# Graph attention: the larger slope moved from exponentials to VectorE, one exponential in place, and shares scaled on ScalarE

## The chip, the cores and the metric

The kernel is one program on one core of a Trainium2 chip. Its metric is the device time in microseconds (us) of one execution. It is a whole network in one launch; the change touches one stage, the attention of the first graph layer.

## The reference, cut to what matters

The first graph layer has 12 heads of 64 values, 1250 nodes and 20,000 edges. For every edge it takes a score `a1[src] + a2[dst]`, a leaky ReLU with slope 0.2, a softmax over the edges that end in one node, and the sum of the source nodes' values by these weights.

```python
ft = jnp.einsum('nhd,ed->nhe', hh, W_fc)
a1 = jnp.einsum('nhd,hd->nh', ft, attn_l)
a2 = jnp.einsum('nhd,hd->nh', ft, attn_r)
e = jax.nn.leaky_relu(a1[src] + a2[dst], negative_slope=NEG_SLOPE)
m = jax.ops.segment_max(e, dst, num_segments=n)
ee = jnp.exp(e - m[dst])
denom = jax.ops.segment_sum(ee, dst, num_segments=n)
alpha = ee / denom[dst]
agg = jax.ops.segment_sum(alpha[:, :, None] * ft[src], dst, num_segments=n)
res = jnp.einsum('nhd,ed->nhe', hh, W_res)
return jax.nn.relu((res + agg).reshape(n, H * D))
```

Behind it come a mixture of experts, two more graph layers and a transformer block, none of which the change touches.

## The kernel before

The edges are kept as a dense table of counts, `counts_u`, source by destination. The nodes make 10 tiles of 125 (`TP`), so a step `i` is one head and one tile of 125 sources against all 1250 destinations: 12 x 10 = 120 steps, in order of heads. The function is `attend_narrow`; its queues are written out by hand, one for each engine, with semaphores between them.

For each step, ScalarE makes two exponentials of 125x1250, one for each slope of the leaky ReLU (lines 1709 and 1710): the row of the destinations plus a bias for each source, `ks` for the slope 1 and `ks_low` for the slope 0.2. Since the exponential rises, the larger of the two results is the exponential of the leaky ReLU. VectorE takes that larger one (`larger`, line 1722), then limits it to 1 and multiplies it by the counts (line 1742). TensorE multiplies the weights by the values with a column of ones (65 columns in all, line 1674), in three pieces of up to 512 destinations, and adds up over the 10 steps of a head in PSUM (`acc`). VectorE's loop takes the larger one of step i+1 before it weighs step i.

The sums of a head are divided by their last column one head later. ScalarE copies them out of PSUM (`copy_sums`, after step 3 of the next head), TensorE turns them by 10 transposes (`turn_sums`, after step 5, line 1662), and VectorE does the rest after step 7 in `take_out`: it adds 1e-16 (1728), inverts (1730), scales all 10 tiles in one instruction (1731) and adds the shares to the result (1735). The last head's sums go the same way behind the last step.

Buffers: 5 for the high slope, 4 for the low one. Two heads' rows and the exponentials of the first two steps are made ahead, in the stage before (`EarlyHeads`). SyncE loads the rows of head h once the exponentials of head h-2 are done, and between them issues 39 fills of zeros for a later stage.

Of the kernel before, what the change touches and what calls it, by code (L numbers as in the profile page):

```python
# [12 lines left out]
ALU = mybir.AluOpType  # L13
ACT = mybir.ActivationFunctionType
# [1536 lines left out]
class EarlyHeads:  # L1551
# [8 lines left out]
    def __init__(self, s, g, tag, ks, ks_low):  # L1560
        self.g, self.ks, self.ks_low = g, ks, ks_low
        G = self.HEADS
        self.rows_all = [s.sb(f"{tag}_rows{i}", [P, 2, N]) for i in range(G)]
        self.lowb_all = [s.sb(f"{tag}_lowb{i}", [P, N]) for i in range(self.STEPS)]
        self.shifted = s.sb(f"{tag}_early_shifted", [TP, NT, 2, G])
        masks = g.far_u[:, :, :].rearrange("p t n -> p (t n)").bitcast(F32)
        self.high = [masks[:, i * N:(i + 1) * N] for i in range(NT // 2)]
# [38 lines left out]
def attend_narrow(g, tag, ks, ks_low, shifted, ft, res, early):  # L1606
# [3 lines left out]

    H = ks.shape[2]
    WIDTH = ft.shape[3]
    DV = WIDTH - 1
    pieces = [(0, 512), (512, 1024), (1024, N)]
    steps = [(h, t) for h in range(H) for t in range(NT)]

    COPY, TURN, TAKE = 3, 5, 7
    HALF = NT // 2  # L1620
    with ExitStack() as ctx:
        s = Scope(g, ctx)
        rows_all = early.rows_all
        rows = [x[0:TP, :, :] for x in rows_all]

        shiftedT = s.sb(f"{tag}_shiftedT", [2 * H, N])[:, :]

        high = early.high
        lowb = [x[0:TP, :] for x in early.lowb_all] + [s.sb(f"{tag}_lowb{i}", [TP, N])[:, :] for i in range(early.STEPS, 4)]
        HB, LB = len(high), len(lowb)  # L1630
# [7 lines left out]
        exp_done, max_done, wts_done = early.exp_done, s.sem(f"{tag}_max"), s.sem(f"{tag}_wts_done")  # L1638
        multiplied, sums_out, sums_turned = s.sem(f"{tag}_multiplied"), s.sem(f"{tag}_sums_out"), s.sem(f"{tag}_sums_turned")
        taken, v_chain = s.sem(f"{tag}_taken"), s.sem(f"{tag}_vc")  # L1640
# [6 lines left out]
        wts = high  # L1647

        @block.tensor
        def _(pe):  # L1650
            for t in range(NT):
                last = pe.transpose(acc[1][0:2 * H, t // 4, (t % 4) * TP:(t % 4 + 1) * TP],
                                    shifted[:, t, :, :].rearrange("p a c -> p (a c)"), g.ident[0:TP, 0:TP])
            last.then_inc(turned, 1)

            def turn_sums(h):
                pe.wait_ge(sums_out, h + 1)
                if h >= 1:

                    pe.wait_ge(taken, h)  # L1660
                for d in range(NT):
                    last = pe.transpose(back[:, d // HALF, (d % HALF) * WIDTH:(d % HALF + 1) * WIDTH],
                                        sumsT[:, d * TP:(d + 1) * TP], g.ident[0:WIDTH, 0:WIDTH])
                last.then_inc(sums_turned, 1)

            for i, (h, t) in enumerate(steps):
                if t == 0 and h == 1:
                    pe.wait_ge(copied, 2)
                if t == 0 and h >= 2:

                    pe.wait_ge(sums_out, h - 1)
                pe.wait_ge(wts_done, i + 1)
                for b, (c0, c1) in enumerate(pieces):
                    last = pe.matmul(acc[h % 2][0:WIDTH, b, 0:c1 - c0], ft[:, t, h, :], wts[i % HB][:, c0:c1],  # L1674
                                     start=(t == 0), stop=(t == NT - 1))
                last.then_inc(multiplied, 1)
                if t == TURN and h >= 1:
                    turn_sums(h - 1)
            turn_sums(H - 1)

        @block.scalar
        def _(act):
            def copy_shifted():
                act.wait_ge(turned, 1)
                act.activation(shiftedT[:, 0:8 * TP].rearrange("p (a b) -> p a b", a=2), acc[1][0:2 * H, 0:2, 0:4 * TP],
                               ACT.Copy).then_inc(copied, 1)
                act.activation(shiftedT[:, 8 * TP:N], acc[1][0:2 * H, 2, 0:2 * TP], ACT.Copy).then_inc(copied, 1)

            def copy_sums(h):
                act.wait_ge(multiplied, (h + 1) * NT)  # L1690
# [6 lines left out]
            for i, (h, t) in enumerate(steps):  # L1697
                if i < early.STEPS:
                    continue
                if i == early.STEPS + 4:  # L1700
                    copy_shifted()
                if t == 0:
                    act.wait_ge(rows_in[h % 2], h // 2 * 16 + 16)
                if i >= HB:

                    act.wait_ge(multiplied, i - HB + 1)
                if i >= LB:
                    act.wait_ge(max_done, i - LB + 1)
# [3 lines left out]
                if t == COPY and h >= 1:  # L1712
                    copy_sums(h - 1)
            copy_sums(H - 1)

        @block.vector
        def _(dve):
            link = chain(dve, v_chain)

            def larger(i):  # L1720
                dve.wait_ge(exp_done, i + 1)
                dve.tensor_tensor(high[i % HB], high[i % HB], lowb[i % LB],  # L1722
                                  op=ALU.max).then_inc(max_done, 1)

            def take_out(h):
                dve.wait_ge(sums_turned, h + 1)
                by_tile = back[:, :, 0:HALF * WIDTH].rearrange("p a (d w) -> p a d w", w=WIDTH)
                link(dve.tensor_scalar(recip[:, :].rearrange("p (a d) -> p a d", a=2), by_tile[:, :, :, DV], 1e-16, None,
                                       op0=ALU.add))
                link(dve.reciprocal(recip[:, :], recip[:, :]))  # L1730
                link(dve.tensor_tensor(shares[:, :, :].rearrange("p (a d) w -> p a d w", a=2), by_tile[:, :, :, 0:DV],
                                       recip[:, :].rearrange("p (a d) -> p a d", a=2).unsqueeze(3)
                                       .to_broadcast([TP, 2, HALF, DV]), op=ALU.mult))
                at = slice(h * DV, (h + 1) * DV)
                dve.tensor_tensor(res[:, :, at], res[:, :, at], shares[:, :, :], op=ALU.add).then_inc(taken, 1)

            larger(0)
            for i, (h, t) in enumerate(steps):
                if i + 1 < len(steps):
                    larger(i + 1)  # L1740
                dve.wait_ge(max_done, i + 1)
                dve.scalar_tensor_tensor(out=wts[i % HB], in0=high[i % HB], scalar=1.0,  # L1742
                                         in1=g.counts_u[:, t, :], op0=ALU.min, op1=ALU.mult).then_inc(wts_done, 1)
                if t == TAKE and h >= 1:
                    take_out(h - 1)
            take_out(H - 1)
            dve.wait_ge(taken, H)

        @block.sync
        def _(sp):  # L1750
# [1 line left out]
            sp.dma_start(g.rows_dram[0:2 * H, :], shiftedT).then_inc(rows_out, 16)  # L1752
            sp.wait_ge(rows_out, 16)
            for h in range(early.HEADS, H):
                sp.wait_ge(exp_done, (h - 1) * NT)
# [268 lines left out]
def gat_layer(g, x, src, dst, etype, w_fc, w_res, attn_l, attn_r, layers, weights):  # L2024
# [9 lines left out]
    with ExitStack() as ctx:  # L2034
# [6 lines left out]
        with ExitStack() as inner:  # L2041
# [8 lines left out]
            early = EarlyHeads(si, g, "gat2", ks, ks_low)  # L2050
            with ExitStack() as inmost:
                sm = Scope(g, inmost)
                row = [x[:, :].unsqueeze(1) for x in early.lowb_all] + [sm.sb("gat_row2", [P, 1, N])[:, :, :]]
# [1367 lines left out]
```

## Time and profile before

| | us |
|---|---|
| time, median of 3 runs | 3122.57 |
| the three runs | 3122.57, 3121.82, 3135.45 |
| the profiled execution: its span, first to last instruction | 3130.0 |
| the attention stage in it, VectorE's first to last instruction | 489.91 to 849.41 |

The profile gives the span of its execution and no separate whole time. Only the longest of the three runs is longer than that span, by 5.4 us; the median lies 7.4 us under the span.

How to read the views: a row of the groups gives the line, the engine, what is written from what, the shape, the count, then busy us and the mean ns of one, then the engine's idle time just before these instructions and what ended it. PE is TensorE's matmul, DVE VectorE, ACT ScalarE. PEclk is TensorE's granted clock as a share of its higher level.

### The profile page before, as it was taken

To read this page: it belongs to the slowest core of one execution; us is meant where nothing else is said; L and a number is where in the kernel's file an instruction comes from. 1 tells how busy PE (TensorE), PEld (TensorE's weight loads), DVE (VectorE), ACT (ScalarE), POOL (GpSimd) and SP (SyncE) were. 2 spreads that over 40 slices of the span, in tenths; PEclk is the share of its full clock that TensorE was granted. 3 is DMA by queue.
4 is the path that set the end of the run, shared out by engine and by line. 5 is a ranking of instruction groups with operands and counts; after the bars stand their busy time and mean duration, and the time that the engine had idled before them with its cause. 6 is when DMAs were issued, how large, how long until landed. Compare 5 with 4: busy or idle time off the path is not lost. (4 is left out here: it accounts for less than half of the span.)

```text
span 3130.0 us, 34859 instructions
## 1 busy us (share of the span) xinstructions
PE 2710.3 (87%) x12638; PEld 2001.7 (64%) x12639; DVE 2038.7 (65%) x2833; ACT 1247.1 (40%) x1499; POOL 293.7 (9%) x148
## 2 busy tenths in 40 slices
PE   7877986888766983999999996999999799999979
PEld 3556982333235981555999995998887655566654
DVE  6765999999853544893888995705677871114451
ACT  1573227889520001111777782225655610004310
POOL 0000000000025853000000001510000000000020
PEclk9998558999867996999999997999999899999979
DMA  1566544211026635542665543625343601000031
GB/s 66 145 176 150 167 147 176 88 49 50 0 75 196 206 135 186 191 147 109 187 175 158 132 113 104 193 79 182 120 130 111 194 14 61 31 5 26 1 90 50
DMA packets 155542, 361.24 MB, mean 115 GB/s; under 512 B 27292, under 2 KB 77924, under 8 KB 154634
## 3 DMA queue, kind: packets, MB, share of 16 engines
q1 hardware_dynamic: 110468, 269.91, 28.6%
q10 hardware_dynamic: 35968, 73.97, 6.8%
q0 software_dynamic: 8960, 15.41, 1.9%
q8 instruction: 93, 1.52, 0.2%
q14 instruction: 53, 0.43, 0.0%
HBM read 276.26 MB, written 82.93 MB: 115 GB/s over the span
## 5 line engine op out<-in xcount | busy, mean ns | idle before, releaser
L1674 PE MATMUL gat_acc<-far_u,gat_ft 125*65 125x512 f32 x720 | 286.7, 540 | 56.1 <-DVE far_u L1742 55.6
L1674 PEld LDWEIGHTS gat_acc<-far_u,gat_ft 125*65 125x65 f32 x720 | 94.1, 142 | 244.9 <-issue 152.8
L1134 PE MATMUL rg_out<-rg_w,rg_hT 128*125 128x384 f32 x720 | 234.3, 489 | 0.0
L2263 PE MATMUL rg2a_acc<-rg2a_value_part,rg2a_wts_part 125*125 125x512 f32 x600 | 204.9, 342 | 14.8 <-DVE rg2a_wts_part L1983 11.4
L2264 PE MATMUL rg2a_acc<-rg2a_value_part,rg2a_wts_part 125*125 125x512 f32 x600 | 205.7, 343 | 0.0
L2265 PE MATMUL rg2a_acc<-rg2a_value_part,rg2a_wts_part 125*125 125x512 f32 x600 | 204.1, 340 | 0.0
L1134 PEld LDWEIGHTS rg_out<-rg_w,rg_hT 128*125 128x125 f32 x720 | 135.8, 189 | 97.4 <-issue 1.5
L1722 DVE TENSOR_TENSOR far_u<-far_u,gat_lowb 125x1250 f32<-125x1250 f32 x120 | 174.3, 1453 | 0.4 <-PEq L782 0.4
L1742 DVE SCALAR_TENSOR_TENSOR far_u<-far_u,counts_u 125x1250 f32<-125x1250 f32 x120 | 174.3, 1453 | 0.0
L1709 ACT ACTIVATE far_u<-gat_rows,gat_ks 125x1250 f32<-125x1250 f32 x118 | 156.7, 1328 | 43.2 <-PE gat_acc L1674 34.2
L365 PE MATMUL sums<-src_hot,key_hot 125*125 125x512 bf16 (+1 forms) x618 | 139.4, 355 | 30.0 <-DVE key_hot L300 28.6
L1710 ACT ACTIVATE gat_lowb<-gat_rows,gat_ks_low 125x1250 f32<-125x1250 f32 x118 | 156.3, 1325 | 0.0
L299 DVE TENSOR_SCALAR src_hot<-number,srcT 125x1250 bf16<-125x1250 uint16 x206 | 112.5, 546 | 44.6 <-PE sums L365 27.0
L1980 DVE TENSOR_TENSOR rg2a_value_part<-rg2a_values,rg2a_value_part 125x770 fp32r<-125x770 f32 x89 | 85.5, 961 | 77.7 <-ACT rg2a_value_part L1933 76.9
L2263 PEld LDWEIGHTS rg2a_acc<-rg2a_value_part,rg2a_wts_part 125*125 125x125 f32 x600 | 112.9, 188 | 30.6 <-DVE rg2a_value_part L1980 12.0
L2263 PE MATMUL rg_out<-rg_w,rg_hT 128*125 128x384 f32 x360 | 123.0, 342 | 8.0 <-POOL rg_w L1210 8.0
L365 PEld LDWEIGHTS sums<-src_hot,key_hot 125*125 125x125 bf16 x618 | 72.4, 138 | 84.9 <-DVE key_hot L300 65.0
L1417 PE MATMUL rg1a_acc<-rg_values,rg1a_high 125*125 125x193 f32 x720 | 122.4, 327 | 3.7 <-DVE rg1a_high L1496 1.9
L1417 PE MATMUL rg1a_acc<-rg1a_values,rg1a_high 125*125 125x193 f32 x720 | 122.1, 327 | 1.7 <-DVE rg1a_high L1496 0.9
L2265 PE MATMUL rg_out<-rg_w,rg_hT 128*125 128x384 f32 x360 | 122.6, 340 | 0.0
L2264 PE MATMUL rg_out<-rg_w,rg_hT 128*125 128x384 f32 x360 | 122.5, 340 | 0.0
L2265 PEld LDWEIGHTS rg2a_acc<-rg2a_value_part,rg2a_wts_part 125*125 125x125 f32 x600 | 113.1, 189 | 14.2
(481 smaller groups left out, 6014.7 us busy)
## 6 DMA issues: line engine op xcount, KB each, us to landing
rg2a_values<-values_dram SPq DMA_DIRECT2D x89, 384.0 KB, 3.4
rg1a_counts<-counts_dram SPq DMA_DIRECT2D x26, 820.3 KB
rg_mask<-far_dram SPq DMA_DIRECT2D x60, 312.5 KB, 3.6
moe_raw<-in_L_ffn_w SPq DMA_DIRECT2D x16, 1152.0 KB, 5.8
relw_chunk<-in_L_gnn_W ACTq DMA_DIRECT2D x36, 384.0 KB, 3.1
gat_rows<-rows_dram SPq DMA_DIRECT2D x10, 1250.0 KB, 5.7
sorted_dram<-gat_zeros SPq DMA_DIRECT2D x30, 384.0 KB, 9.4
values_dram<-rg_stage ACTq DMA_DIRECT2D x30, 384.0 KB, 2.3
```

Of the source, the lines that this page charges most:

```text
L299: dve.tensor_scalar(src_hot[u][:, :], number[:, 0:N], srcT[:, bass.ds(t, 1)], None, op0=ALU.is_equal)
L365: last = pe.matmul(sums_flat[b][:, 512 * k:512 * k + w], key_hot[u][:, :], src_hot[u][:, 512 * k:512 * k + w], start=start, stop=False, sk ...
L1134: last = pe.matmul(self.out_ps[n % 2][:, a, 0:384], self.hT[:, c, t * TP:(t + 1) * TP], self.w_sb[r % 2][:, c, a * 384:(a + 1) * 384], sta ...
L1417: last = pe.matmul(tile_of(h, d), wts[i % HB][:, d * TP:(d + 1) * TP], stream[i % VB][:, :], start=first and d % 2 == 0, stop=final, skip_ ...
L1674: last = pe.matmul(acc[h % 2][0:WIDTH, b, 0:c1 - c0], ft[:, t, h, :], wts[i % HB][:, c0:c1], start=(t == 0), stop=(t == NT - 1))
L1709: act.activation(high[i % HB], rows[h % 2][:, 0, :], ACT.Exp, bias=ks[:, t, h:h + 1])
L1710: act.activation(lowb[i % LB], rows[h % 2][:, 1, :], ACT.Exp, bias=ks_low[:, t, h:h + 1]).then_inc(exp_done, 1)
L1722: dve.tensor_tensor(high[i % HB], high[i % HB], lowb[i % LB], op=ALU.max).then_inc(max_done, 1)
L1742: dve.scalar_tensor_tensor(out=wts[i % HB], in0=high[i % HB], scalar=1.0, in1=g.counts_u[:, t, :], op0=ALU.min, op1=ALU.mult).then_inc(wts ...
L2263: pe.matmul(out, still[0], moving[0], start=first, stop=False)
L2264: pe.matmul(out, still[0], moving[1], start=False, stop=False)
L2265: return pe.matmul(out, still[1], moving[0], start=False, stop=final)
```

## The change

Four things are done together.

- VectorE now makes the exponent: for each step it adds `ks_high` = 0.8 x `ks` to the high row, by a pointer scalar (one value for each partition), and takes the larger of that and the low row (`exponents`). ScalarE makes one exponential of it, in place, with the bias `ks_low`, instead of two.
- Two steps make a pair. The counts are multiplied over the pair in one instruction of 125x2500, and TensorE is told of a pair at a time, so there are 60 pairs, 5 for each head. The ring has 4 buffers of a pair. The first pair's exponentials are still those made ahead.
- The scaling of the sums moves from VectorE (one instruction of 125x640, line 1731) to ScalarE: ten copies from PSUM of 64 columns each, with a pointer scale (`share`). `take_out` is parted into `invert`, after pair 3 of the next head, and the addition, after pair 4. ScalarE's `share` stands after the exponentials of pair 3 in its queue.
- The places are counted in pairs: the sums are copied after pair 1, turned after pair 2.

SyncE's wait before a row load is now on VectorE's exponents, since it is VectorE that reads the rows.

```diff
-        high = early.high
-        lowb = [x[0:TP, :] for x in early.lowb_all] + [s.sb(f"{tag}_lowb{i}", [TP, N])[:, :] for i in range(early.STEPS, 4)]
+        ks_high = s.sb(f"{tag}_ks_high", [TP, NT, H])
+        ring = early.pairs + [s.sb(f"{tag}_pair", [TP, 2, N])[:, :, :], early.lowb_pair[0:TP, :, :]]
+        RING = len(ring)
...
-    COPY, TURN, TAKE = 3, 5, 7
+    pairs = [(h, 2 * u) for h in range(H) for u in range(HALF)]
+    COPY, TURN, TAKE = 1, 2, 3
...
-            for i, (h, t) in enumerate(steps):
+            for i, (h, t) in enumerate(pairs):
...
                 pe.wait_ge(wts_done, i + 1)
-                for b, (c0, c1) in enumerate(pieces):
-                    last = pe.matmul(acc[h % 2][0:WIDTH, b, 0:c1 - c0], ft[:, t, h, :], wts[i % HB][:, c0:c1],
-                                     start=(t == 0), stop=(t == NT - 1))
+                for u in range(2):
+                    for b, (c0, c1) in enumerate(pieces):
+                        last = pe.matmul(acc[h % 2][0:WIDTH, b, 0:c1 - c0], ft[:, t + u, h, :], ring[i % RING][:, u, c0:c1],
+                                         start=(t + u == 0), stop=(t + u == NT - 1))
                 last.then_inc(multiplied, 1)
-                if t == TURN and h >= 1:
+                if t == 2 * TURN and h >= 1:
                     turn_sums(h - 1)
...
+            def share(h):
+                act.wait_ge(inverted, h + 1)
+                if h >= 1:
+                    act.wait_ge(taken, h)
+                for d in range(NT):
+                    o = (d % HALF) * WIDTH
+                    last = act.activation(shares[:, d, :], back[:, d // HALF, o:o + DV], ACT.Copy,
+                                          scale=recip[:, d:d + 1])
+                last.then_inc(shared, 1)
...
-                act.activation(high[i % HB], rows[h % 2][:, 0, :], ACT.Exp, bias=ks[:, t, h:h + 1])
-                act.activation(lowb[i % LB], rows[h % 2][:, 1, :], ACT.Exp,
-                               bias=ks_low[:, t, h:h + 1]).then_inc(exp_done, 1)
+                for u in range(2):
+                    act.wait_ge(max_done, 2 * i + u)
+                    x = ring[i % RING][:, u, :]
+                    act.activation(x, x, ACT.Exp, bias=ks_low[:, t + u, h:h + 1]).then_inc(exp_done, 1)
+                if t == 2 * COPY and h >= 1:
+                    copy_sums(h - 1)
+                if t == 2 * TAKE and h >= 1:
+                    share(h - 1)
...
+            def exponents(i):
+                h, t = pairs[i]
+                if t == 0:
+                    dve.wait_ge(rows_in[h % 2], h // 2 * 16 + 16)
+                if i >= RING:
+                    dve.wait_ge(multiplied, i - RING + 1)
+                for u in range(2):
+                    dve.scalar_tensor_tensor(out=ring[i % RING][:, u, :], in0=rows[h % 2][:, 0, :],
+                                             scalar=ks_high[:, t + u, h:h + 1], in1=rows[h % 2][:, 1, :],
+                                             op0=ALU.add, op1=ALU.max).then_inc(max_done, 1)
...
+            for i, (h, t) in enumerate(pairs):
+                if i + 1 < len(pairs):
+                    exponents(i + 1)
+                if i == 0:
+                    dve.wait_ge(max_done, 1)
+                else:
+                    dve.wait_ge(exp_done, 2 * i)
+                dve.scalar_tensor_tensor(out=ring[i % RING], in0=ring[i % RING], scalar=1.0,
+                                         in1=g.counts_u[:, t:t + 2, :], op0=ALU.min, op1=ALU.mult).then_inc(wts_done, 1)
+                if t == 2 * TAKE and h >= 1:
+                    invert(h - 1)
+                if t == 2 * TAKE + 2 and h >= 1:
+                    take_out(h - 1)
```

`invert` is the addition of 1e-16 and the reciprocal of the old `take_out`, behind a wait on the turned sums; the new `take_out` is the addition to the result, behind a wait on `shared`.

## Rows read from the trace of the kernel before

**Rows 1.** The first line of the profile page, whole program.

```profile
span 3130.0 us, 34859 instructions
```

**Rows 2.** Groups by line and shape, 485 to 860 us, all engines.

```profile
L1674 PE MATMUL gat_acc<-far_u,gat_ft 125*65 125x512 f32 x480 | 242.3, 629 | 56.1 <-DVE far_u L1742 55.6
L1722 DVE TENSOR_TENSOR far_u<-far_u,gat_lowb 125x1250 f32<-125x1250 f32 x120 | 174.3, 1453 | 0.4 <-PEq L782 0.4
L1742 DVE SCALAR_TENSOR_TENSOR far_u<-far_u,counts_u 125x1250 f32<-125x1250 f32 x120 | 174.3, 1453 | 0.0
L1709 ACT ACTIVATE far_u<-gat_rows,gat_ks 125x1250 f32<-125x1250 f32 x118 | 156.7, 1328 | 43.2 <-PE gat_acc L1674 34.2 <-PEq L782 7.9 <-issue 0.9
...
L1694 ACT ACTIVATE gat_sumsT<-gat_acc 65x1250 f32<-65x1250 f32 x12 | 14.4, 1200 | 12.9 <-PE gat_acc L1674 12.9
L1731 DVE TENSOR_TENSOR gat_shares<-gat_back,gat_recip 125x640 f32<-125x640 f32 x12 | 9.9, 825 | 0.4
```

**Rows 3.** Waits, 485 to 860 us: total us, times, longest.

```profile
ACT far_u L1709 <- PE gat_acc L1674: 34.2, 18, 3.8
...
DVE gat_recip L1728 <- PE gat_back L1662: 5.7, 1, 5.7
```

**Rows 4.** Timeline of head 3: start and duration in us, engine, line.

```profile
585.86 1.45 DVE L1722 TENSOR_TENSOR far_u<-far_u,gat_lowb 125x1250 f32<-125x1250 f32 x1
...
587.23 1.45 DVE L1742 SCALAR_TENSOR_TENSOR far_u<-far_u,counts_u 125x1250 f32<-125x1250 f32 x1
...
588.61 1.45 DVE L1722 TENSOR_TENSOR far_u<-far_u,gat_lowb 125x1250 f32<-125x1250 f32 x1
...
594.22 2.31 PE L1674 MATMUL gat_acc<-far_u,gat_ft 125*65 125x512 f32 x6 [0.43 <-DVE far_u L1742]
...
596.37 1.21 PE L1662 MATMUL gat_back<-ident,gat_sumsT 65*125 65x65 f32 x10
...
599.57 0.16 DVE L1728 TENSOR_SCALAR gat_recip<-gat_back 125x10 f32<-125x10 f32 x1
...
599.76 0.22 DVE L1730 RECIPROCAL gat_recip<-gat_recip 125x10 f32<-125x10 f32 x1
...
601.62 1.45 DVE L1722 TENSOR_TENSOR far_u<-far_u,gat_lowb 125x1250 f32<-125x1250 f32 x1
...
604.50 2.32 PE L1674 MATMUL gat_acc<-far_u,gat_ft 125*65 125x512 f32 x6 [2.48 <-DVE far_u L1742]
```

**Rows 5.** Timeline of the stage's end, same columns.

```profile
838.71 2.82 DVE L1742 SCALAR_TENSOR_TENSOR far_u<-far_u,counts_u 125x1250 f32<-125x1250 f32 x2
...
840.21 4.42 PE L1674 MATMUL gat_acc<-far_u,gat_ft 125*65 125x512 f32 x12 [2.48 <-DVE far_u L1742]
...
848.58 0.82 DVE L1735 TENSOR_TENSOR gat_res<-gat_res,gat_shares 125x640 f32<-125x640 f32 x1
```

**Rows 6.** Timeline of ScalarE, short reads of PSUM, no pointer operand.

```profile
387.44 0.21 ACT L1085 ACTIVATE score_weights<-relw_out 128x48 f32<-128x48 f32 x1 [4.90 <-PE relw_out L1065]
...
387.55 0.31 ACT L1085 ACTIVATE score_weights<-relw_out 128x48 f32<-128x48 f32 x2
```

**Rows 7.** Timeline of ScalarE: one without, two with a pointer bias.

```profile
2162.03 0.60 ACT L1935 ACTIVATE rg2a_wts_part<-rg2a_high 125x500 fp32r<-125x500 f32 x1
2162.54 0.70 ACT L1918 ACTIVATE rg_high<-rgat_h,rg_ks 125x500 f32<-125x500 f32 x1
2163.14 0.70 ACT L1919 ACTIVATE rg_lowb<-rgat_h,rg_ks_low 125x500 f32<-125x500 f32 x1
```

**Rows 8.** Groups of VectorE by line, whole program: pointer scalar, immediate.

```profile
L2963 DVE SCALAR_TENSOR_TENSOR x_all<-x_all,pick_score 125x1250 f32<-125x1250 f32 x10 | 15.2, 1521 | 0.4
...
L2063 DVE SCALAR_TENSOR_TENSOR x_all<-gat_res,x_all 125x768 f32<-125x768 f32 x10 | 8.8, 951 | 0.5 <-PEq L1621 0.5
```

**Rows 9.** Windows of two heads: PE, PEld, DVE, ACT, POOL, PEclk, DMA.

```profile
545.50:549.50 4.00, 3.93 (x7) 1.34 (x8) 4.00 (x4) 0.32 (x1) 0.00 (x0) 0.57 1.03 416
...
603.50:608.00 4.50, 3.08 (x8) 1.07 (x9) 4.50 (x4) 2.39 (x3) 0.00 (x0) 1.00 0.00 0
```

More of the change, by code:

```diff
@@ L1563, in __init__ @@
         self.rows_all = [s.sb(f"{tag}_rows{i}", [P, 2, N]) for i in range(G)]
-        self.lowb_all = [s.sb(f"{tag}_lowb{i}", [P, N]) for i in range(self.STEPS)]
+        self.lowb_pair = s.sb(f"{tag}_lowb", [P, self.STEPS, N])
+        self.lowb_all = [self.lowb_pair[:, i, :] for i in range(self.STEPS)]
         self.shifted = s.sb(f"{tag}_early_shifted", [TP, NT, 2, G])
         masks = g.far_u[:, :, :].rearrange("p t n -> p (t n)").bitcast(F32)
-        self.high = [masks[:, i * N:(i + 1) * N] for i in range(NT // 2)]
+        self.pairs = [masks[:, i * N:(i + 2) * N].rearrange("p (u n) -> p u n", u=2) for i in (0, 2)]
+        self.high = [self.pairs[0][:, i, :] for i in range(self.STEPS)]
         self.rows_in, self.exp_done = s.sems(f"{tag}_rows_in", G), s.sem(f"{tag}_exp")
@@ L1616, in attend_narrow @@
     pieces = [(0, 512), (512, 1024), (1024, N)]
-    steps = [(h, t) for h in range(H) for t in range(NT)]
-    COPY, TURN, TAKE = 3, 5, 7
     HALF = NT // 2
+    pairs = [(h, 2 * u) for h in range(H) for u in range(HALF)]
+    COPY, TURN, TAKE = 1, 2, 3
     with ExitStack() as ctx:
@@ L1637, in attend_narrow @@
         rows_in = early.rows_in
-        exp_done, max_done, wts_done = early.exp_done, s.sem(f"{tag}_max"), s.sem(f"{tag}_wts_done")
+        early_exp, max_done, exp_done = early.exp_done, s.sem(f"{tag}_max"), s.sem(f"{tag}_exp_done")
+        wts_done, scaled = s.sem(f"{tag}_wts_done"), s.sem(f"{tag}_ks_scaled")
         multiplied, sums_out, sums_turned = s.sem(f"{tag}_multiplied"), s.sem(f"{tag}_sums_out"), s.sem(f"{tag}_sums_turned")
+        inverted, shared = s.sem(f"{tag}_inverted"), s.sem(f"{tag}_shared")
         taken, v_chain = s.sem(f"{tag}_taken"), s.sem(f"{tag}_vc")
@@ L1645, in attend_narrow @@
         block = s.block()
-        wts = high
         @block.tensor
@@ L1660, in turn_sums @@
                     pe.wait_ge(taken, h)
+                    pe.wait_ge(shared, h)
                 for d in range(NT):
@@ L1682, in _ @@
         def _(act):
[L1683 to L1687, printed above, removed]
+            act.activation(ks_high[:, :, :], ks[:, :, :], ACT.Copy, scale=0.8).then_inc(scaled, 1)
+            act.wait_ge(turned, 1)
+            act.activation(shiftedT[:, 0:8 * TP].rearrange("p (a b) -> p a b", a=2), acc[1][0:2 * H, 0:2, 0:4 * TP],
+                           ACT.Copy).then_inc(copied, 1)
+            act.activation(shiftedT[:, 8 * TP:N], acc[1][0:2 * H, 2, 0:2 * TP], ACT.Copy).then_inc(copied, 1)
             def copy_sums(h):
-                act.wait_ge(multiplied, (h + 1) * NT)
+                act.wait_ge(multiplied, (h + 1) * HALF)
                 if h >= 1:
@@ L1695, in copy_sums @@
                                ACT.Copy).then_inc(sums_out, 1)
-            for i, (h, t) in enumerate(steps):
-                if i < early.STEPS:
-                    continue
[L1700 to L1708, printed above, removed]
-                act.activation(high[i % HB], rows[h % 2][:, 0, :], ACT.Exp, bias=ks[:, t, h:h + 1])
-                act.activation(lowb[i % LB], rows[h % 2][:, 1, :], ACT.Exp,
-                               bias=ks_low[:, t, h:h + 1]).then_inc(exp_done, 1)
-                if t == COPY and h >= 1:
+            def share(h):
[9 more added lines that the diff above has]
+                if i == 0:
+                    continue
+                for u in range(2):
[3 more added lines that the diff above has]
+                if t == 2 * COPY and h >= 1:
                     copy_sums(h - 1)
+                if t == 2 * TAKE and h >= 1:
+                    share(h - 1)
             copy_sums(H - 1)
+            share(H - 1)
         @block.vector
@@ L1718, in _, with invert @@
             link = chain(dve, v_chain)
[L1720 to L1725, printed above, removed]
+            def exponents(i):
[8 more added lines that the diff above has]
+                                             op0=ALU.add, op1=ALU.max).then_inc(max_done, 1)
+            def invert(h):
                 dve.wait_ge(sums_turned, h + 1)
+                if h >= 1:
+                    dve.wait_ge(shared, h)
                 by_tile = back[:, :, 0:HALF * WIDTH].rearrange("p a (d w) -> p a d w", w=WIDTH)
@@ L1729, in take_out @@
                                        op0=ALU.add))
[L1730 to L1733, printed above, removed]
+                dve.reciprocal(recip[:, :], recip[:, :]).then_inc(inverted, 1)
+            def take_out(h):
                 at = slice(h * DV, (h + 1) * DV)
+                dve.wait_ge(shared, h + 1)
                 dve.tensor_tensor(res[:, :, at], res[:, :, at], shares[:, :, :], op=ALU.add).then_inc(taken, 1)
[L1737 to L1744, printed above, removed]
+            dve.wait_ge(early_exp, early.STEPS)
+            dve.tensor_tensor(ring[0], ring[0], early.lowb_pair[0:TP, :, :], op=ALU.max).then_inc(max_done, 1)
+            dve.wait_ge(scaled, 1)
+            for i, (h, t) in enumerate(pairs):
+                if i + 1 < len(pairs):
+                    exponents(i + 1)
+                if i == 0:
+                    dve.wait_ge(max_done, 1)
[6 more added lines that the diff above has]
+                if t == 2 * TAKE + 2 and h >= 1:
                     take_out(h - 1)
+            invert(H - 1)
             take_out(H - 1)
@@ L1754, in _ @@
             for h in range(early.HEADS, H):
-                sp.wait_ge(exp_done, (h - 1) * NT)
+                sp.wait_ge(max_done, 2 * ((h - 1) * HALF - 1) + 1)
                 src = bass.AP(tensor=g.rows_dram.tensor, offset=h * N, ap=[[0, P], [H * N, 2], [1, N]])
@@ L2052, in gat_layer @@
                 sm = Scope(g, inmost)
-                row = [x[:, :].unsqueeze(1) for x in early.lowb_all] + [sm.sb("gat_row2", [P, 1, N])[:, :, :]]
+                row = [x.unsqueeze(1) for x in early.lowb_all] + [sm.sb("gat_row2", [P, 1, N])[:, :, :]]
                 greatest(g, "gat", H, 1, row, None, ks, qd, ks_low, shifted,
```

1 line of the change is left out of this document (removed).

## The prediction, made before the changed kernel had run

> **What bounds the kernel now.** The change is inside one stage, so I read that stage and nothing else as the bound. In the grouped lines of 485 to 860 us the reader is to see two columns, the mean of one and the idle time ahead. VectorE's two instructions of a step have 120 x 1.453 us each and an idle time of 0.4 and 0.0 us; TensorE has idled 56.1 us for VectorE's weights, and ScalarE 34.2 us for TensorE to give buffers back [rows 2, 3]. The list of waits says the same from the other side: VectorE's only wait above a microsecond in the stage is the one of 5.7 us at its very end, for the last turned sums [rows 3]. So VectorE sets the pace, ScalarE has room, TensorE a little.
>
> The timeline then gives the pitch, which is less than the duration: one VectorE instruction starts 1.37 us after the one before while each lasts 1.45 [rows 4], an overlap of 0.08. A step is 2 x 1.371 = 2.742 us. Taking a head out costs VectorE 599.57 to 601.62 = 2.05 us [rows 4]. 120 x 2.742 + 11 x 2.05 = 351.6 us, and the trace has 841.53 - 489.91 = 351.6 from its first instruction to the end of the last weights (838.71 + 2.82, [rows 5]; 489.91 from the table). The bound is thus closed: nothing but VectorE's own work stands in it. ScalarE's second exponential, which the change takes away, is off this path.
>
> **The change part by part.** *VectorE's own work.* The exponent is the same width as the old maximum, but has a pointer scalar. The row nearest is L2963, the same shape and operation with a pointer, 1.521 us against 1.453 with an immediate [rows 2, 8]: pitch 1.439. I take it; the other end is 1.371, if the pointer were free. The counts over a pair: 768 columns last 0.951 and 1250 last 1.453 us [rows 2, 8], 1.0415 ns a column, so 2500 last 2.755, pitch 2.673. A pair is 2 x 1.439 + 2.673 = 5.551 us against 5.484 for two steps. The saved fixed cost (0.07) is more than paid back by two pointers (0.14). Over the stage, with the first pair's maximum as one wide instruction: 2.673 + 118 x 1.439 + 60 x 2.673 = 332.9 against 329.0, or **+3.9**.
>
> Taking out: the addition of 1e-16 and the reciprocal stay, 0.19 to the reciprocal's start [rows 4] and 0.22 - 0.08 = 0.14 more, 0.33 us; the addition to the result keeps 0.74 (0.82 - 0.08). The scaling goes and the waits around it. 0.33 + 0.74 = 1.07 against 2.05, for 11 heads **-10.8**; the last of these additions now comes behind the last weights and so leaves the path, **-0.7**. VectorE alone would gain 7.6 us.
>
> *The wait that comes with `share`.* This is the step that decides. ScalarE's queue has, in each head from the second on, exponentials of pair 3, ten shares, exponentials of pair 4. The shares wait for `inverted`, which VectorE gives only after it has made the exponents of pair 4 and weighed pair 3. So the exponents of pair 4 lie ready and ScalarE stands still in front of the shares; behind it wait the exponentials of pair 4, and for them VectorE. Count from the start of `invert`. Reciprocal done at 0.19 + 0.22 = 0.41, ScalarE starts at 0.47. (The 0.06 is a hand-over: weights ready at 838.71 + 1.45 = 840.16, TensorE at 840.21 [rows 5]; I take it for every one.) Price of a share: PSUM reads of 48 columns without a pointer come every 0.11 and 0.10 us [rows 6], 0.12 for 64 columns at 0.83 ns a column; a pointer adds 0.60 - 0.51 = 0.09 to the pitch for equal width [rows 7]: 0.216, ten are 2.16. Then two exponentials, pitch 1.23 and duration 1.33 (L1709, [rows 2]; the pitch is the duration less 0.10, as in [rows 7]). 0.47 + 2.16 + 1.23 + 1.33 + 0.06 = 5.25. VectorE in the meantime does 0.33 + 2 x 1.439 = 3.21, the exponents of the next pair. It then waits 2.04 us. Ten times **+20.4**. In the last head there are no exponents left to make: 5.25 - 0.33 = **+4.9**.
>
> Bounds of a share: 0.12 (the pointer free) and 0.315 (full duration of one: 0.21 + 0.01 + 0.09, no overlap). The row is between them because its parts are measured in this trace; the ends move the whole by -11.6 and +11.8. The Trainium skill, page "ScalarE: Activation LUTs", section "What ACT_TABLE_LOAD costs", has 186 ns plus 0.833 ns a column, 93 ns for each pointer operand, and an overlap of 93 ns back to back. By that a share of 64 columns would be 0.239 us and the sum 28.6 instead of 26.0. The trace's 0.09 for the pointer agrees; its 0.10 us for 48 columns is under the page's 0.133.
>
> *The turned sums.* Before, the turn stood two steps ahead of VectorE's reading; now it is one pair, and TensorE must first finish pair 2. Count from the end of pair 2's weights: 0.06, the pair 2 x 2.31 = 4.62 (in rows 4 one step is 2.31), then the turn. After a step's end at 594.22 + 2.31 = 596.53 the turn ends at 596.37 + 1.21 = 597.58 [rows 4], 1.05 more, and 0.06: 5.79. VectorE wants them at 2 x 1.439 + 2.673 - 0.08 = 5.47. It waits 0.32, eleven times **+3.5**. If TensorE is late by 1 us there, each microsecond costs 11; if it overlaps the turn's start a little, this falls to 0.
>
> *TensorE.* 4.62 of 5.55 us in each pair, so it holds. Before pair 4 of each head it now idles: weights of pair 3 at 0 (the start of `invert`), TensorE is done at about 4.6, the next weights come at 5.25 + 2.76 + 0.06 = 8.07, so 3.5 us. After idle stretches of 2.48 us [rows 4] the granted clock was 0.57 in one head's stretch of 4 us and 1.00 in another's [rows 9]: 1.2 GHz at times, and 2.4 at others. With 3.5 I expect 1.2 GHz after each. A mean of 0.57 over 4 us is 2 x 0.43 x 4 = 3.4 us at the lower level, in which 1.7 us of work is lost. TensorE has 0.9 us of room in each pair and 1.7 in the next one (5.55 + 0.74 - 4.62), before the next turn reads its place; it is hidden in all heads but the last.
>
> *The end.* From the last weights to TensorE's end it was 840.21 + 4.42 - 841.53 = 3.10 us [rows 5]; now 0.06 + 4.62 + 1.7 (clock) = 6.38, **+3.3**. Scaling the last sums: 0.06 + 2.16 + 0.10 + 0.06 = 2.38 against 0.82 and a hand-over in the queue, about 0.88, **+1.5**. ScalarE's copy and the turn are unchanged.
>
> *At nothing.* The first weights are ready 8.2 us after the start and not 4.2, hidden since VectorE never stops for TensorE. `ks_high` is one small instruction on ScalarE while VectorE takes its first maximum; without cover 0.3 us. `copy_sums` waits for TensorE's last pair of a head, 6.4 us after its weights with the low clock, and lasts 1.2 [rows 2]; the exponents that it could hold up are ready at 0.74 + 5.55 + 1.5 = 7.8, and VectorE asks for them another 4 us later. The row loads wait for exponents made at about the time of the exponentials before. The ring of 4 pairs asks TensorE to be less than about 6 us late.
>
> Sum: 3.9 - 10.8 - 0.7 + 20.4 + 4.9 + 3.5 + 3.3 + 1.5 = **+26.0 us**, made against the span of 3130.0 [rows 1], which becomes 3156.0. The median of the runs lies 7.4 under that span; I put the same sum on it: 3122.6 + 26.0 = **3148.6**.
>
> **The rivals.** *Not slower: ScalarE's shares don't hold it up.* The mechanism is the same queue, the price the 25.3 us of waits. From 0.47 to VectorE's need at 3.21 there are 2.74 us, and two exponentials with the hand-over take 2.62; so this needs ten shares in 0.12 us. Without these waits the stage has 26.0 - 25.3 = +0.7, or 3123.3; even with the turn's wait gone too, 3119.8. For it speaks only that ScalarE, with one exponential fewer, is idle half of the time; against it that it is idle at the wrong place. 4%.
>
> *Cheaper prices.* A share at 0.12 and a pointer scalar at nothing on VectorE: the waits shrink by 0.96 a head and grow by 0.14 with the shorter exponents; by the same sum +9, or 3131.6. With the share alone +14.1, or 3136.7. 12%, most of it within 0.5%.
>
> *TensorE late at the turn.* If it stays at 1.2 GHz into pair 2 of the next head, or the turn doesn't overlap, 1 us a head: 11 more, +37, or 3160. For it: the idle stretches grow from 2.48 to 3.5 us. Against: in [rows 9] 1.2 GHz lasts one stretch. 12%.
>
> *The change doesn't do what it says:* ScalarE's work is halved, but VectorE's isn't. That is part of my forecast. A faster one would need more than one column a cycle for the wide instruction; L1742 with the same types has one column in 1.04 ns [rows 2]. By half of 160 us it would be some 3070. 2%.
>
> **How the numbers follow.** Forecast 70%, with its own range 3143 to 3154. Range for 8 in 10: from cheaper shares, 3136, to the late turn, 3160, and a microsecond for the spread of the runs: 3135 to 3161. What can be told from no change is 0.5%, 15.6 us, so the border is 3138.2. Slower: forecast, late turn and a few hundredths of the cheap case, 0.83. Same: 0.14. Faster: 0.03.
>
> **What would show it.** L1731's place taken by ten short ScalarE copies a head at about 0.32 us each, starting 0.22 apart. VectorE's wide instruction with an idle time ahead of some 25 us in all, released by ScalarE's exponential, eleven times, the longest 4.9; 3 us more ahead of the addition of 1e-16, released by the turn. Exponents at 1.52 us. TensorE's longest idle 3.5 us and 1.2 GHz behind it. The prediction is wrong if VectorE's idle time in the stage is under 10 us, or if the turn's wait is above 1 us a head.

## The result, and the profile after

The changed kernel takes 3149.5 us (median of four runs, 3144.8 to 3150.4) against 3124.6 for the one before: a ratio of 1.0069, 95% interval 1.0049 to 1.0089. (The medians alone would give 1.0080, the means of the same runs 1.0070.) It is slower, and inside the range. The profiled execution has a span of 3148.6 us against 3130.0 [rows 1]; its own time is 3150.39, so 1.8 us lie around the span, so the one profiled of the kernel before took about 3131.8, some 7 us over its median.

One number carries the comparison better than the whole: the stage, from VectorE's first instruction to the end of the last addition to the result. It went from 489.91 to 849.41, 359.5 us, to 489.41 to 869.61, **380.2 us: +20.7**. The rest of the profile, in which nothing was changed, came out 2 us shorter.

The groups of the stage after the change (columns as in [rows 2]; the ring's other two tiles have rows of their own, with equal durations):

```profile
L1739 DVE SCALAR_TENSOR_TENSOR far_u<-gat_rows,gat_ks_high 125x1250 f32<-125x1250 f32 x58 | 85.2, 1509 | 0.0
L1767 DVE SCALAR_TENSOR_TENSOR far_u<-far_u,counts_u 125x2500 f32<-125x2500 f32 x30 | 82.6, 2754 | 9.3 <-ACT far_u L1719 9.3
L1719 ACT ACTIVATE far_u<-far_u,gat_ks_low 125x1250 f32<-125x1250 f32 x58 | 76.8, 1356 | 39.4 <-DVE far_u L1739 37.5
...
L1709 ACT ACTIVATE gat_shares<-gat_back,gat_recip 125x64 f32<-125x64 f32 x120 | 25.9, 338 | 82.2 <-DVE gat_recip L1750 82.2
...
L1755 DVE TENSOR_TENSOR gat_res<-gat_res,gat_shares 125x640 f32<-125x640 f32 x12 | 9.8, 818 | 2.2 <-ACT gat_shares L1709 2.2
```

VectorE's instructions have 1.509 and 2.754 us, ScalarE has 120 copies of 0.338. What was 0.0 in the column of idle time [rows 2] is now 9.3 us ahead of the counts, ended by ScalarE's exponential. The list of waits has it for all three tiles of the ring, and ScalarE's own wait in front of the shares:

```profile
ACT gat_shares L1709 <- DVE gat_recip L1750: 82.2, 12, 7.3
...
DVE far_u L1767 <- ACT far_u L1719: 9.3, 5, 1.9
DVE gat_lowb L1767 <- ACT gat_lowb L1719: 8.4, 3, 4.7
DVE gat_recip L1748 <- PE gat_back L1666: 8.1, 1, 8.1
...
DVE gat_pair L1767 <- ACT gat_pair L1719: 5.6, 3, 1.9
```

9.3 + 8.4 + 5.6 = 23.3 us, eleven times. ScalarE stands still for 82.2 us in front of the shares, up to 7.3 at a time. In the head shown below, the first exponents behind the shares are ready for the last 4.6 of these 7.3 us (from 597.87 + 1.51). One head in the timeline:

```profile
592.33 2.95 DVE L1739 SCALAR_TENSOR_TENSOR gat_pair<-gat_rows,gat_ks_high 125x1250 f32<-125x1250 f32 x2
...
595.20 2.75 DVE L1767 SCALAR_TENSOR_TENSOR far_u<-far_u,counts_u 125x2500 f32<-125x2500 f32 x1
...
597.87 2.94 DVE L1739 SCALAR_TENSOR_TENSOR gat_lowb<-gat_rows,gat_ks_high 125x1250 f32<-125x1250 f32 x2
...
598.00 4.42 PE L1679 MATMUL gat_acc<-far_u,gat_ft 125*65 125x512 f32 x12 [1.12 <-DVE far_u L1767]
...
600.73 2.75 DVE L1767 SCALAR_TENSOR_TENSOR gat_pair<-gat_pair,counts_u 125x2500 f32<-125x2500 f32 x1
...
602.26 1.20 PE L1666 MATMUL gat_back<-ident,gat_sumsT 65*125 65x65 f32 x10
603.50 0.17 DVE L1748 TENSOR_SCALAR gat_recip<-gat_back 125x10 f32<-125x10 f32 x1
...
603.70 0.22 DVE L1750 RECIPROCAL gat_recip<-gat_recip 125x10 f32<-125x10 f32 x1
603.84 2.90 DVE L1739 SCALAR_TENSOR_TENSOR far_u<-gat_rows,gat_ks_high 125x1250 f32<-125x1250 f32 x2
603.95 2.16 ACT L1709 ACTIVATE gat_shares<-gat_back,gat_recip 125x64 f32<-125x64 f32 x10 [7.30 <-DVE gat_recip L1750]
...
605.94 2.62 ACT L1719 ACTIVATE gat_lowb<-gat_lowb,gat_ks_low 125x1250 f32<-125x1250 f32 x2
...
608.59 2.76 DVE L1767 SCALAR_TENSOR_TENSOR gat_lowb<-gat_lowb,counts_u 125x2500 f32<-125x2500 f32 x1 [1.86 <-ACT gat_lowb L1719]
611.27 0.82 DVE L1755 TENSOR_TENSOR gat_res<-gat_res,gat_shares 125x640 f32<-125x640 f32 x1
...
611.41 6.11 PE L1679 MATMUL gat_acc<-gat_lowb,gat_ft 125*65 125x512 f32 x12 [3.46 <-DVE gat_lowb L1767]
```

The reader is to follow one chain. `invert` (603.50, 603.70) lets the shares go at 603.95. Ten of them hold ScalarE to 605.94, and only then come the two exponentials of `gat_lowb`, whose exponents VectorE had made from 597.87 to 600.81. VectorE is done with the next exponents at 606.7, waits, and multiplies the counts at 608.59. In all ten heads the wait is 1.86 us in the profile, 1.94 with the lost overlap of 0.08. TensorE is left without weights for 3.46 us, and its next pair lasts 6.11 instead of 4.42 us, in this head and in the ten others that have shares before pair 4. The window over that pair has a granted clock of 0.72, that is 2 x 0.28 x 6.1 = 3.4 us at 1.2 GHz, as long as in [rows 9]:

```profile
611.40:617.50 6.10, 6.09 (x12) 2.04 (x12) 6.10 (x4) 2.67 (x2) 0.00 (x0) 0.72 0.00 0
```

The end of the stage, to be held against [rows 5]:

```profile
854.56 2.76 DVE L1767 SCALAR_TENSOR_TENSOR gat_lowb<-gat_lowb,counts_u 125x2500 f32<-125x2500 f32 x1 [4.67 <-ACT gat_lowb L1719]
...
857.38 6.11 PE L1679 MATMUL gat_acc<-gat_lowb,gat_ft 125*65 125x512 f32 x12 [3.45 <-DVE gat_lowb L1767]
...
866.59 2.16 ACT L1709 ACTIVATE gat_shares<-gat_back,gat_recip 125x64 f32<-125x64 f32 x10 [1.85 <-DVE gat_recip L1750]
868.78 0.83 DVE L1755 TENSOR_TENSOR gat_res<-gat_res,gat_shares 125x640 f32<-125x640 f32 x1 [2.23 <-ACT gat_shares L1709]
```

The last weights are done at 857.32, TensorE at 863.49, 6.2 us later instead of 3.1, and the last addition waits for ten shares.

### The profile page after: what moved, and what is told of

It reads as the page before. It is cut to its first block and busy times, and to the rows that moved or that the text cites. A ratio compares the mean times of both kernels' runs of the same rounds, so it can differ in the third digit from the quotient of the medians.

```text
span 3148.6 us, 34707 instructions
## 1 busy us (share of the span) xinstructions
PE 2706.7 (86%) x12638; PEld 2006.1 (64%) x12639; DVE 2033.3 (65%) x2760; ACT 1134.3 (36%) x1502; POOL 291.7 (9%) x148
## 5 line engine op out<-in xcount | busy, mean ns | idle before, releaser
L1679 PE MATMUL gat_acc<-far_u,gat_ft 125*65 125x512 f32 x360 | 143.0, 550 | 39.2 <-DVE far_u L1767 38.7
L1679 PEld LDWEIGHTS gat_acc<-far_u,gat_ft 125*65 125x65 f32 x360 | 49.9, 145 | 130.7 <-issue 81.6
L2291 PEld LDWEIGHTS rg2a_acc<-rg2a_value_part,rg2a_wts_part 125*125 125x125 f32 x600 | 112.9, 188 | 30.6 <-DVE rg2a_value_part L2008 12.0
L2293 PEld LDWEIGHTS rg2a_acc<-rg2a_value_part,rg2a_wts_part 125*125 125x125 f32 x600 | 113.0, 188 | 14.1
L1417 PEld LDWEIGHTS rg1a_acc<-rg_values,rg1a_high 125*125 125x125 f32 x720 | 118.0, 188 | 6.1 <-DMA rg_values<-values_dram 3.7
L2292 PEld LDWEIGHTS rg2a_acc<-rg2a_value_part,rg2a_wts_part 125*125 125x125 f32 x600 | 112.8, 188 | 13.9
L1417 PEld LDWEIGHTS rg1a_acc<-rg1a_values,rg1a_high 125*125 125x125 f32 x720 | 118.1, 188 | 2.7 <-DMA rg1a_values<-values_dram 1.5
L987 DVE CUSTOM_DVE_ANT_0 rg_lowb<-rgat_h,rg_mask 125x1250 f32<-125x1250 f32 x80 | 110.7, 1454 | 12.3 <-DMA rgat_h<-rows_dram 12.3
```

Source lines behind the costliest of these rows:

```text
L987: dve.tensor_tensor_reduce(out=junk[i % 2], in0=row[n % RB][0:TP, k, :], in1=far, scale=1.0, scalar=3 * FAR, op0=ALU.subtract, op1=ALU.max ...
L1417: last = pe.matmul(tile_of(h, d), wts[i % HB][:, d * TP:(d + 1) * TP], stream[i % VB][:, :], start=first and d % 2 == 0, stop=final, skip_ ...
L1679: last = pe.matmul(acc[h % 2][0:WIDTH, b, 0:c1 - c0], ft[:, t + u, h, :], ring[i % RING][:, u, c0:c1], start=(t + u == 0), stop=(t + u == ...
L2291: pe.matmul(out, still[0], moving[0], start=first, stop=False)
L2292: pe.matmul(out, still[0], moving[1], start=False, stop=False)
L2293: return pe.matmul(out, still[1], moving[0], start=False, stop=final)
```

## The experiments

All times of stages are from each kernel's one profiled execution; within it equal parts repeat to some hundredths of a microsecond, as the wait of 1.86 us does. Whole times of one kernel lie up to 22 us apart, and what is left of the span without the stage goes from 2759 to 2782 us over the nine profiles, so ratios are given with their intervals, each against runs of the kernel before taken beside it.

**1. The shares later in ScalarE's queue.** One line of the changed kernel:

```diff
-                if t == 2 * TAKE and h >= 1:
+                if t == 2 * TAKE + 2 and h >= 1:
                     share(h - 1)
```

> The changed kernel with one edit: in ScalarE's queue the ten shares stand behind the exponentials of pair 4, not in front of them. Nothing is left out. My theory (the shares block exponentials whose input is ready): VectorE's waits of 1.9 us in ten heads and 4.8 us in the last one, 24 us in all, go away, and TensorE's idle stretch before pair 4 shrinks from 3.5 to about 1.6 us, so that its clock may stay up for the last pair (1.7 us more). The stage, from VectorE's first instruction to the last addition to the result, falls from 380.2 to about 354 us, and the time to 3149.5 - 26 = 3124, level with the kernel before (359.5 us of stage) or up to 5 us faster. Rival (the new waits come from the turned sums or from TensorE, and the shares only fill them): the stage stays above 375 us and the time above 3145.

Measured: stage 355.4 us, ratio to the kernel before 0.9982 (0.9972 to 0.9992). A head in its timeline:

```profile
572.00 0.22 DVE L1750 RECIPROCAL gat_recip<-gat_recip 125x10 f32<-125x10 f32 x1
572.13 2.90 DVE L1739 SCALAR_TENSOR_TENSOR gat_lowb<-gat_rows,gat_ks_high 125x1250 f32<-125x1250 f32 x2
572.25 2.15 ACT L1709 ACTIVATE gat_shares<-gat_back,gat_recip 125x64 f32<-125x64 f32 x10 [1.77 <-DVE gat_recip L1750]
...
574.23 2.63 ACT L1719 ACTIVATE gat_lowb<-gat_lowb,gat_ks_low 125x1250 f32<-125x1250 f32 x2
...
574.95 2.76 DVE L1767 SCALAR_TENSOR_TENSOR gat_pair<-gat_pair,counts_u 125x2500 f32<-125x2500 f32 x1
...
577.62 0.82 DVE L1755 TENSOR_TENSOR gat_res<-gat_res,gat_shares 125x640 f32<-125x640 f32 x1
```

The shares start 0.03 us behind the reciprocal, as in the changed kernel, but the exponentials of pair 4 are done by then; VectorE goes from its exponents (572.13) to the counts (574.95) without idle time. No wait of VectorE for ScalarE is left in the stage but the last addition's. TensorE's idle stretch before pair 4 fell from 3.46 to 1.95 us; the pair behind it lasts 4.39 us in six heads and 6.08 in the four others. One line took back 24.8 us, more than the 20.7 that the whole change had cost: the place of the shares is the cause. The rival (the turned sums or TensorE make the waits) falls.

**2. The scaling back on VectorE.** Pairs and exponents stay, and ScalarE's shares go.

```diff
...
+                link(dve.reciprocal(recip[:, :], recip[:, :]))
+                link(dve.tensor_tensor(shares[:, :, :].rearrange("p (a d) w -> p a d w", a=2), by_tile[:, :, :, 0:DV],
+                                       recip[:, :].rearrange("p (a d) -> p a d", a=2).unsqueeze(3)
+                                       .to_broadcast([TP, 2, HALF, DV]), op=ALU.mult))
+                take_out(h)
...
```

> The changed kernel with the scaling of the sums undone: VectorE scales all ten tiles in one instruction and adds them at once, after pair 3, as in the kernel before; pairs and the exponent on VectorE stay. Nothing is left out. My theory: ScalarE's blocking goes (-24 us), VectorE takes 11 x (2.05 - 1.07) = 11 us more, and the tail loses 1.5 us of short shares: stage about 366 us, 6 to 7 us above the kernel before, made up of the pointer scalars (+3), the wait for the turned sums (+1) and TensorE's longer last pair (+3). Time about 3131. Rival (pairs and the exponent are themselves worth a gain, as their fewer instructions suggest): stage below 359.

Measured: stage 365.1, ratio 1.0023 (1.0012 to 1.0034).

```profile
L1735 DVE SCALAR_TENSOR_TENSOR far_u<-gat_rows,gat_ks_high 125x1250 f32<-125x1250 f32 x58 | 85.4, 1515 | 0.0
L1764 DVE SCALAR_TENSOR_TENSOR far_u<-far_u,counts_u 125x2500 f32<-125x2500 f32 x30 | 82.7, 2756 | 0.0
...
L1745 DVE TENSOR_TENSOR gat_shares<-gat_back,gat_recip 125x640 f32<-125x640 f32 x12 | 9.9, 825 | 0.4
```

The waits are gone here too, and what is left is what pairs and exponent are worth alone: 5.6 us of loss; the rival, that they are worth a gain, falls. To the last weights it is 355.7 us against 351.6, and the tail 9.3 against 7.9.

**3. The shares made twice.** The first ten go to a spare tile.

```diff
-                for d in range(NT):
+                for k in range(2 * NT):
+                    d = k % NT
                     o = (d % HALF) * WIDTH
-                    last = act.activation(shares[:, d, :], back[:, d // HALF, o:o + DV], ACT.Copy,
+                    last = act.activation((spare if k < NT else shares)[:, d, :], back[:, d // HALF, o:o + DV], ACT.Copy,
```

> The changed kernel with each of the ten shares made twice, the first time into a spare tile, so that ScalarE's part of a head takes 2.0 us more. The output is the same. My theory: nothing covers the shares, so each microsecond of them is a microsecond of wait on VectorE: 11 heads and the tail x 2.0 = 24 us more, stage about 404 us, time about 3173. Rival (the wait is set by something else and the shares are partly hidden): less than 12 us more.

Measured: stage 405.7, 25.5 more than the changed kernel; time 3166.7, ratio 1.0126 (1.0109 to 1.0144).

```profile
577.18 2.70 ACT L1721 ACTIVATE gat_lowb<-gat_lowb,gat_ks_low 125x1250 f32<-125x1250 f32 x2
577.47 2.76 DVE L1769 SCALAR_TENSOR_TENSOR gat_pair<-gat_pair,counts_u 125x2500 f32<-125x2500 f32 x1 [3.90 <-ACT gat_pair L1721]
...
580.28 0.29 PEld L1680 LDWEIGHTS gat_acc<-gat_pair,gat_ft 125*65 125x65 f32 x2 [5.89 <-DVE gat_pair L1769]
```

The wait went from 1.86 to 3.90 us in each head, by 2.04 us: the ten added shares take 1.96, and the exponential that VectorE waits for, behind them, lasts 1.48 instead of 1.40 us. Nothing covers either, they count one to one. The stage has 1 us more than 12 x 2.04, since TensorE, behind 5.5 us of idle time, now ends 7.2 us after the last weights instead of 6.2. The whole time, of two runs only, moved by 17 us where the stage moved by 25.5, and 3173 was expected: a miss. In the profile the rest of the program is 9 us shorter than in the changed kernel's, and no run here says why.

**4. The pointer scalar.** On the first experiment's kernel, `scalar=ks_high[...]` becomes `scalar=0.5`. The kernel then leaves out the source's part of the slope 1, so its output is not that of the reference; shapes and semaphores are the same.

> The late shares of the first experiment, and the pointer scalar of VectorE's exponent replaced by a constant (0.5), which leaves the source's score out of the slope 1; shapes and waits are the same. My theory (the exponent costs more than the old maximum for its pointer alone): 118 instructions go from a pitch of 1.432 to 1.371 us, VectorE's work and with it the stage falls by 7.2 us, from 355.4 to 348.2. Rival (the operation or the reading of two rows costs it, the pointer nothing): the stage stays at 355.

Measured: stage 349.4, 6.0 less than with the pointer; ratio 0.9953 (0.9940 to 0.9967).

```profile
L1739 DVE SCALAR_TENSOR_TENSOR far_u<-gat_rows 125x1250 f32<-125x1250 f32 x58 | 81.7, 1450 | 0.0
```

The pointer costs 1.431 against 1.371 us of pitch, by the distances between starts; that is 0.06 for each of 118, 7.1 us. VectorE then asks for the turned sums earlier and waits 0.12 us more in each head (2.888 instead of 2.770 from the start of the counts to the addition of 1e-16): 1.3 us go back. The operation and its two rows cost nothing more than the old maximum, which had the same pitch of 1.371.

**5. Late shares, and the end of the stage shortened.** The last pair is weighed and multiplied step by step.

```diff
-                pe.wait_ge(wts_done, i + 1)
                 for u in range(2):
+                    pe.wait_ge(wts_done, i + 1 + (u if i == len(pairs) - 1 else 0))
...
+                for a, b in (((0, 2),) if i < len(pairs) - 1 else ((0, 1), (1, 2))):
```

The last head's sums are also scaled on VectorE in one instruction.

> The late shares of the first experiment, and two edits at the stage's end: the very last pair is weighed and multiplied step by step, and the last head's sums are scaled by VectorE in one instruction. Nothing is left out. My theory: against the first experiment TensorE ends 2.1 us earlier and the last scaling takes 1.5 us less, so the stage is about 350 us, 9 us under the kernel before, and the time about 3116, a ratio of 0.997 to it. Rival (the end of the stage is covered by something else, or the waits come back elsewhere): no better than the kernel before.

Measured: stage 354.1, ratio 0.9975 (0.9965 to 0.9985). Half a miss: 1.3 us came from the scaling, nothing from the last pair.

```profile
826.04 1.20 PE L1666 MATMUL gat_back<-ident,gat_sumsT 65*125 65x65 f32 x10
...
827.32 4.42 PE L1679 MATMUL gat_acc<-gat_pair,gat_ft 125*65 125x512 f32 x12
...
827.62 2.77 DVE L1767 SCALAR_TENSOR_TENSOR gat_lowb<-gat_lowb,counts_u 125x1250 f32<-125x1250 f32 x2
...
831.58 4.36 PE L1679 MATMUL gat_acc<-gat_lowb,gat_ft 125*65 125x512 f32 x12
```

With no exponents left to make, VectorE has the last weights ready (827.62 + 2.77) while TensorE is still in the pair before: turn, pair and pair follow each other without a gap from 826.04 to 835.94. There TensorE is the bound, and earlier weights help nobody.

**6. One part alone, on the kernel before.** Steps, two exponentials and the maximum stay; only the scaling moves, to where ScalarE's queue really is by then; the last head's is left on VectorE.

```diff
+                if t == 1 and h >= 2:
+                    share(h - 2)
                 if t == COPY and h >= 1:
                     copy_sums(h - 1)
+            share(H - 2)
             copy_sums(H - 1)
...
                 if t == TAKE and h >= 1:
-                    take_out(h - 1)
+                    invert(h - 1)
+                if t == NT - 1 and h >= 1:
+                    take_out(h - 1)
```

> The kernel before, with one part of the change alone: steps, two exponentials and the maximum stay, and the scaling of the sums goes to ScalarE as ten shares, placed where its queue really is by then, behind the exponentials of step 1 of the head after; VectorE inverts after step 7 and adds after step 9; the last head is scaled by VectorE. Nothing is left out. My theory (the move is the part that pays, the rest costs): VectorE has 11 x (2.05 - 1.07) = 10.8 us less, ScalarE just fits (20 x 1.23 + 1.1 + 2.0 = 27.7 us of 28.5 a head), so the stage is about 349 us, 10 to 11 under the kernel before and 5 under the late shares with pairs; ratio 0.9965. Rival (ScalarE, which now has 97% of the time of a head, becomes the bound, since the buffers that it waits for come late): VectorE waits 1 us or more in each head and the stage is 359 or above.

Measured: stage **347.3**, ratio 0.9971 (0.9961 to 0.9982). The stage is the shortest of all kernels that compute the whole, 12.2 us under the one before and 32.9 under the changed one. The expected 10.8 lacked two things: the last of the eleven additions now comes behind the last weights (0.7), and the maximum behind each reciprocal has a pitch 0.055 us shorter (0.6).

```profile
L1766 DVE SCALAR_TENSOR_TENSOR far_u<-far_u,counts_u 125x1250 f32<-125x1250 f32 x120 | 174.2, 1452 | 0.0
L1737 DVE TENSOR_TENSOR far_u<-far_u,gat_lowb 125x1250 f32<-125x1250 f32 x120 | 173.6, 1447 | 0.4 <-PEq L782 0.4
...
L1705 ACT ACTIVATE gat_shares<-gat_back,gat_recip 125x64 f32<-125x64 f32 x110 | 23.5, 329 | 3.4 <-DVE gat_recip L1747 3.4
```

VectorE's column of idle time is again 0.0 and 0.4, and the list of waits has nothing of ScalarE's work against it, full as ScalarE is (busy for 326 of the 345 us from 490 to 835). The timeline shows why: ScalarE had run ahead, so the reciprocal of 595.62 was long there when the shares came at 598.04, and the addition follows them at 601.18.

```profile
595.62 0.22 DVE L1747 RECIPROCAL gat_recip<-gat_recip 125x10 f32<-125x10 f32 x1
...
596.82 1.32 ACT L1722 ACTIVATE gat_lowb<-gat_rows,gat_ks_low 125x1250 f32<-125x1250 f32 x1
...
598.04 2.13 ACT L1705 ACTIVATE gat_shares<-gat_back,gat_recip 125x64 f32<-125x64 f32 x10
...
600.01 1.40 ACT L1721 ACTIVATE far_u<-gat_rows,gat_ks 125x1250 f32<-125x1250 f32 x1
...
601.18 0.82 DVE L1759 TENSOR_TENSOR gat_res<-gat_res,gat_shares 125x640 f32<-125x640 f32 x1
```

**7. The counts by step.** The first experiment's kernel, counts multiplied and TensorE told step by step.

```diff
...
+                for u in range(2):
+                    last = dve.scalar_tensor_tensor(out=ring[i % RING][:, u, :], in0=ring[i % RING][:, u, :], scalar=1.0,
+                                                    in1=g.counts_u[:, t + u, :], op0=ALU.min, op1=ALU.mult)
+                    last.then_inc(wts_done, 1)
...
```

> The late shares of the first experiment, with the counts multiplied step by step again and TensorE told of each step; the exponent stays. Nothing is left out. My theory (the pair saves one overlap of fixed cost and nothing else): 60 x (2 x 1.371 - 2.672) = 4.2 us more of VectorE, stage 359.6. The wait for the turned sums (0.09 us a head) goes, 1 us less, as TensorE starts a pair 1.4 us earlier: 358.6. Rival (pairs cost more by making TensorE late than they save): stage below 355.

Measured: stage 357.4, 2.0 more than with pairs; ratio 1.0002 (0.9992 to 1.0012). To the last weights 3.4 us more, as worked out (4.2 less most of the 1.0 of turn waits); at the end 1.3 less, since TensorE starts the last pairs a step earlier, which the expectation had left out. The pair is worth 2 us, and the exponent's pointer costs more than that.

## Why the prediction was right, point by point

The sum of the prediction against the trace (of the changed kernel, less that of before):

| step | predicted | trace |
|---|---|---|
| VectorE's own work, last addition off the path | -7.6 | -8.9 |
| wait behind the shares, ten heads | +20.4 | +19.4 |
| the same, last head | +4.9 | +4.8 |
| wait for the turned sums | +3.5 | +1.0 |
| TensorE's end | +3.3 | +3.1 |
| last scaling | +1.5 | +1.3 |
| stage | +26.0 | +20.7 |

- *The blocking shares.* Right in place, mechanism and size: experiment 1 removes it by place alone, experiment 3 moves it one to one. A share had a pitch of 0.20 us against 0.216 (603.95 to 605.94 for ten), 1.99 us a head against 2.16; part of that came back, as the exponential behind the shares lasted 1.40 and not 1.33. The estimate from the figures of the Trainium skill, "ScalarE: Activation LUTs", section "What ACT_TABLE_LOAD costs", was further off at 0.239; by the same figures the duration for 64 columns and one pointer is estimated at 0.332, near the 0.338 of the trace.
- *VectorE's own work.* The gain of this row is what is left of the trace when its waits are taken off. That the pointers cost more than the pair saves was right, and experiments 4 and 7 show both parts. The size was 1.3 us off: the pitch is 1.431, not 1.439, and in ten heads the exponent behind the reciprocal costs only 1.385.
- *The turned sums.* This is the mis-sized term: 0.09 us a head instead of 0.32. I took two steps of TensorE as 2 x 2.31; without a gap between them a pair lasts 4.42, which stood in the last line of TensorE in [rows 5]. That is 0.20 of the 0.23 us. Experiment 4 shows the wait to be real: it grows by 0.12 when VectorE is 0.12 faster a pair.
- *The clock.* 3.5 us of idle time and 1.7 us lost behind it, as measured: 3.46, and 6.11 instead of 4.42. It is hidden in all heads but the last: VectorE's next need of TensorE, the turned sums, comes 2.767 us behind the start of the counts here and 2.770 in experiment 1, where six of ten such pairs lost nothing.
- *The whole time.* That 3148.6 came within 1 us of 3149.5 is luck. The ratio says +21.6 us, the stage +20.7, the sum said 26.0; the median of the kernel before had also moved from 3122.6 to 3124.6 with a fourth run, and the medians of the two kernels lie 24.9 apart.
- *Small slips of the sum.* 332.86 less 329.04 is 3.8 and not 3.9. By its own prices the cheaper share alone gives +14.4 and not +14.1, and a share of 0.239 us gives 28.8 and not 28.6. None of them moves the range.
- *The rivals.* "Not slower" named the right condition from the other side: with ScalarE out of the way the kernel is not slower, experiment 1. I had put the stage at +0.7 then and it is -4.1. The late turn and the cheap share didn't come.

What became of ScalarE's halved exponentials? They gave no gain: the amount of ScalarE's work wasn't the bound, before or after; the place of the shares in its queue was. Experiments 2 and 6 part the change: the exponent and the pairs alone cost 5.6 us, the moved scaling alone gives 12.2 at the right place (9.7 with the pairs, 365.1 to 355.4; up to the last weights it is 12.1 there too, and 2.4 are lost at the end, to ten short shares and TensorE's later end), and costs 15.1 at the place that it was given (365.1 to 380.2).

## What to carry to other kernels

Work moved to an idle engine must be placed where that engine's queue is at that moment: an instruction that waits for its input blocks everything behind it, ready or not, so count where each queue will be, not where its loop index is. Halving the work of an engine that isn't the bound is worth nothing, and each pointer scalar that it puts on the bound is paid for. Where one queue runs ahead by several steps, the moved work costs nothing even with the engine almost full.

## What the runs showed of the hardware

- The VectorE instruction right behind the reciprocal of 10 columns has a pitch of 1.385 us where its like has 1.431 (0.046 less); without a pointer, in experiment 4, it is 1.325 against 1.371, and in experiment 6 the maximum there has 1.316 against 1.371. So it isn't the pointer's doing; no run tells what it is.
- ScalarE's exponentials last 1.356 us in the mean in the changed kernel's row above, against 1.328 [rows 2], and it is not that each is slower. In the changed kernel 76 of the 118 last 1.34 us; the 42 that follow ten shares with no idle time between last 1.39 to 1.41, and in experiment 3, behind twenty shares, 1.47 to 1.49. Back to back their starts lie 1.23 us apart in both kernels. No run tells why the duration grows. VectorE, which waits for the end of one, pays the longer duration: 0.08 of the 2.04 us that experiment 3 added to each wait.
